# Six of POOL's convolution additions per batch issued as accumulating DMA transfers from a product buffer of their own, in a two-layer attention and convolution kernel

## The chip, the cores and the metric

The kernel runs on one core of a Trainium2 chip. The metric is the device time of one execution, in microseconds (us). The engines are PE (matrix products), DVE (vector), ACT (scalar), POOL (GpSimd) and SP, which issues the loads and stores. They run side by side, each through its own list of instructions in order, and meet at semaphores.

## The reference

The input is x, 4 images of 256 channels by 32 x 32 pixels, all float32. Layer one computes per batch image:

```python
q, k, v = h @ wq.T, h @ wk.T, h @ wv.T                      # 768 channels in all
dw = conv(qkv, dw_kernel, 5x5, 'SAME', one filter per channel)
pw = conv(dw, pw_kernel, 1x1, groups of 8 channels)
qkv_all = concat([qkv, pw])                                 # linear attention of 8-channel heads, with relu
out = (scores @ query)[:-1] / (denominator + EPS)
y = batchnorm(conv1x1(out, proj_kernel)) + x
```

Layer two is a full attention over the 1,024 pixels: y is normalized per channel, energy = F^T G (1024 x 1024), softmax over its rows, the result multiplied by H(y), one more 1x1 convolution, plus y. The part that the change touches is `dw`, the depthwise 5 x 5 convolution: 25 taps for each of 768 channels, each a shifted image times one number per channel, added up.

## The kernel before

The 768 channels are six tiles of 128 partitions. `raw` holds the images with a border, `conv` the sums. For each tile 25 taps are to be added up, and they are shared out by tile. DVE does tiles 2, 3, 0 and most of 1 with one multiply-and-add each. For tiles 4 and 5 and for 17 taps of tile 1, ACT writes a product (image times weight) into one of the buffers `prod`, and POOL adds it to a sum. Ten of these 17 (`LATE`) are added to a tile `late` of their own, which lies in `rows`; the other seven are the taps (1, 10) to (1, 16), here called the shared taps. Tap (1, 10) is written straight to `conv` by ACT and starts the sum, and the six others are additions of POOL. DVE takes that sum as the start of its own part, taps (1, 17) to (1, 24).

`POOL_SEQ` is the list of 57 products of a batch: the taps of tiles 4 and 5 in turn, with the shared taps put in at places 32, 34, ..., 44. ACT makes the products in that order, at most `PROD_BUFS` additions ahead of POOL, and POOL adds them in that order. In the first batch PE does tile 5 and ten taps of tile 0 with diagonal matrices (`diagonal_conv`), so that the list `FIRST_POOL_SEQ` is shorter.

The batches overlap. The body of batch b on each engine ends layer one, does layer two and, between its own steps, the convolution of batch b + 1. How many products ACT makes behind each of its steps is written out by hand in tables such as these two, for the eight row blocks (0 to 7) of layer two's softmax:

```python
PRODUCTS_EXP = (2, 3, 4, 1, 1, 2, 1, 0, 0, 1)
PRODUCTS_ATT = (1, 2, 2, 1, 1, 4, 3, 5, 0, 3)
```

In this loop block i goes through `energy` on PE (L533), a row maximum on DVE (L1116), the exponential on ACT (L900), transposes on PE (L546), their copies `pt` on ACT (L909), `values` on PE (L555), and a final operation on DVE (L1133). Products 30 and 31 come after the first exponential, 32 to 34 after the second, 35 after the first pair of `pt` copies, 36 to 39 after the third exponential, 40 and 41 after the second pair of copies, 42 after the fourth exponential, 43 and 44 after the third pair of copies.

PE begins layer one's end (`body`, L578) of a batch only when POOL has done all of its `conv` additions. POOL's nine late additions follow, and PE waits for them before it multiplies `late` (L595).

The order on each engine is the order of the code. No scheduler is between.

Of the kernel before, what the change touches and what calls it, by code (L numbers as in the profile page):

```python
# [6 lines left out]
ALU = mybir.AluOpType  # L7
# [5 lines left out]
P = 128  # L13
# [3 lines left out]
N = SIDE * SIDE  # L17
# [31 lines left out]
SHARED_TILE = 1  # L49
# [3 lines left out]
LATE = 10  # L53
SHARED_TAPS = 7

PROD_BUFS = 5

KV_TILES = (2, 4, 5, 3)
Q_TILES = (0, 1)
# [9 lines left out]
CARRY = 18  # L69


def pool_order(taps):

    own = [(t, i) for i in range(NTAPS) for t in POOL_TILES]
    for i in range(SHARED_TAPS):
        own.insert(SHARED_AT + 2 * i, (SHARED_TILE, LATE + i))
    return [tap for tap in own if tap in taps]
# [4 lines left out]
POOL_SEQ = pool_order(ALL_TAPS)  # L82
FIRST_POOL_SEQ = pool_order([tap for tap in ALL_TAPS if tap not in PE_TAPS])
DVE_SEQ = [(t, i) for t in DVE_TILES for i in range(NTAPS) if (t, i) not in POOL_SEQ + LATE_SEQ]
DVE_TAPS, PRODUCTS = len(DVE_SEQ), len(POOL_SEQ)
# [2 lines left out]
assert DVE_SEQ.index(PE_SHARED_END) < DVE_TAPS - CARRY  # L88

POOL_STARTS = [(t, 0) for t in POOL_TILES] + [(SHARED_TILE, LATE)]  # L90
ADD_SEQ = [tap for tap in POOL_SEQ if tap not in POOL_STARTS]
FIRST_ADD_SEQ = [tap for tap in FIRST_POOL_SEQ if tap not in POOL_STARTS]
POOL_ADDS = len(ADD_SEQ)


# [50 lines left out]
def conv_seq_kernel(nc, x, wqkv, dw, pw, proj, bn, fgw, hw, ow, l1b, masks, out):  # L146
    with ExitStack() as ctx:
        def sb(name, shape, dt=F32):
            return ctx.enter_context(nc.sbuf_tensor(name, shape, dt))

        def sem(name):
            return ctx.enter_context(nc.semaphore(name))
# [7 lines left out]
        conv = sb("conv", [P, TILES, N])  # L160
        rows = sb("rows", [P, ROW_BUFS, N])
        q_raw = sb("q_raw", [P, 2, CK, N])
        prod = sb("prod", [P, PROD_BUFS, N])
        pt = sb("pt", [P, PT_BUFS, NB, P])
        kt = sb("kt", [P, RB, C])
        vt = sb("vt", [P, RB, CK, SCW + 1])
# [79 lines left out]
        bc_part = sem("bc_part")  # L246
        conv_dve = sem("conv_dve")
        prod_ready = sem("prod_ready")
        conv_pool = sem("conv_pool")
        dve_step = sem("dve_step")  # L250
        res_biased = sem("res_biased")
# [46 lines left out]
        def dve_count(b, n):  # L298
            return DVE_TAPS * b + n


        def product_count(b, n):
            return len(FIRST_POOL_SEQ) + (PRODUCTS + LATE) * b - PRODUCTS + n

        def add_count(b, n):
            return len(FIRST_ADD_SEQ) + (POOL_ADDS + LATE - 1) * b - POOL_ADDS + n

# [3 lines left out]
        def late_add_count(b, n):  # L311
            return add_count(b, POOL_ADDS) + n
# [27 lines left out]
        def image_drained(b, t):  # L340

            return (A_AT["raw_q", b] + 2 * (Q_TILES.index(t) + 1) if t in Q_TILES
                    else A_AT["raw_kv", b] + 2 * (KV_TILES.index(t) + 1))

        def conv_read(b, t):

            return A_AT["pwq", b] + A_PWQ if t in Q_TILES else A_AT["pwkv", b] + A_PWKV
# [6 lines left out]
        def square(image):  # L354
            return image.rearrange("p (y x) -> p y x", x=SIDE)
# [387 lines left out]
        def _(act):  # L743
# [20 lines left out]
            def conv_products(b, first, last):  # L764

                seq, adds = (POOL_SEQ, ADD_SEQ) if b else (FIRST_POOL_SEQ, FIRST_ADD_SEQ)
                for n in range(first, min(last, len(seq))):
                    t, i = seq[n]
                    if (t, i) in POOL_STARTS:
                        act.wait_ge(a_free, image_drained(b, t))  # L770
                        if b:
                            act.wait_ge(a_full, conv_read(b - 1, t))
                        dst, part = conv[:, t, :], False
                    else:
                        m = adds.index((t, i))

                        if b:
                            act.wait_ge(conv_pool, add_count(b, max(m - PROD_BUFS + 1, 0)))
                        elif m >= PROD_BUFS:
                            act.wait_ge(conv_pool, m - PROD_BUFS + 1)  # L780
                        dst, part = prod[:, m % PROD_BUFS, :], True
                    product(dst, t, i, part)
# [7 lines left out]
            def late_products(b, first, last):  # L790

                for n in range(first, min(last, LATE)):
                    if n > 0:

                        act.wait_ge(conv_pool, late_add_count(b, max(n - PROD_BUFS, 0)))
                    product(late if n == 0 else prod[:, (n - 1) % PROD_BUFS, :], *LATE_SEQ[n], n > 0)
# [130 lines left out]
            done = [0]  # L927
# [31 lines left out]
        def _(dve):  # L959
# [17 lines left out]
            def conv_taps(b, first, last):  # L977

                for n in range(first, last):
                    t, i = DVE_SEQ[n]  # L980
                    if b == 0 and (t, i) in PE_TAPS:
                        continue
                    if n == 0 or DVE_SEQ[n - 1][0] != t:
                        dve.wait_ge(a_free, image_drained(b, t))
                    if n > 0 or b:

                        skipped = PE_SHARED_TAPS if b == 0 and (t, i) == PE_SHARED_END else 0
                        dve.wait_ge(conv_dve, dve_count(b, n - skipped))
                    if i == NTAPS - 1 and b:
                        dve.wait_ge(a_full, conv_read(b - 1, t))  # L990
                    final = square(conv[:, t, :])
                    if SHARED_TAPS and t == SHARED_TILE and i == LATE + SHARED_TAPS:

                        adds = ADD_SEQ if b else FIRST_ADD_SEQ
                        done = adds.index((t, i - 1)) + 1
                        if n >= DVE_TAPS - CARRY:
                            done = POOL_ADDS if b else len(FIRST_ADD_SEQ)
                        dve.wait_ge(conv_pool, add_count(b, done) if b else done)
                        tap(acc, t, i, final).then_inc(conv_dve, 1)
                    elif b == 0 and (t, i) == PE_SHARED_END:  # L1000

                        dve.wait_ge(a_free, A_AT["conv_shared", 0] + A_CONV)
                        tap(acc, t, i, final).then_inc(conv_dve, 1 + PE_SHARED_TAPS)
                    else:
                        starts = n == 0 or DVE_SEQ[n - 1][0] != t
                        tap(final if i == NTAPS - 1 else acc, t, i, None if starts else acc).then_inc(conv_dve, 1)
# [168 lines left out]
        @block.gpsimd  # L1175
        def _(pool):
            def rstd(b, c):
                pool.wait_ge(var_ready, CK * b + c + 1)
                pool.tensor_tensor(stat_rstd[:, c:c + 1], stat_ve[:, c:c + 1], minus_half[:, c:c + 1],  # L1179
                                   ALU.pow).then_inc(rstd_ready, 1)  # L1180

            def add(total, m, i):

                total, product = inner(square(total), i), inner(square(prod[:, m % PROD_BUFS, :]), i)
                pool.tensor_tensor(total, total, product, ALU.add).then_inc(conv_pool, 1)  # L1185

            def conv_adds(b, first, last):

                seq, adds = (POOL_SEQ, ADD_SEQ) if b else (FIRST_POOL_SEQ, FIRST_ADD_SEQ)
                for m in range(first, min(last, len(adds))):  # L1190
                    t, i = adds[m]
                    n = seq.index((t, i)) + 1
                    pool.wait_ge(prod_ready, product_count(b, n) if b else n)

                    if (t, i - 1) in adds:
                        before = adds.index((t, i - 1)) + 1
                        pool.wait_ge(conv_pool, add_count(b, before) if b else before)
                    add(conv[:, t, :], m, i)

            def late_adds(b):  # L1200

                for m in range(LATE - 1):
                    pool.wait_ge(prod_ready, late_product_count(b, m + 2))
                    if m > 0:
                        pool.wait_ge(conv_pool, late_add_count(b, m))
                    add(late, m, LATE_SEQ[m + 1][1])

            pool.memset(raw[:], 0.0).then_inc(images_cleared, 1)

            pool.wait_ge(constants_set, 1)  # L1210
            pool.wait_ge(bn_ve_ready, 1)
            pool.tensor_tensor(bn_tmp, bn_ve, minus_half, ALU.pow).then_inc(bn_rstd_ready, 1)
            conv_adds(0, 0, 4)
            split_lo(pool, 1)
            conv_adds(0, 4, POOL_ADDS)
            for b in range(B):
                late_adds(b)
                if b + 1 < B:
                    conv_adds(b + 1, 0, RSTD_AT[0])
                rstd(b, 0)  # L1220
                if b + 1 < B:
                    conv_adds(b + 1, RSTD_AT[0], RSTD_AT[1])
                rstd(b, 1)
                if b + 1 < B:
                    conv_adds(b + 1, RSTD_AT[1], POOL_ADDS)
                if b + 2 < B:
                    split_lo(pool, b + 2)
# [51 lines left out]
```

## Time and profile before

| what | value |
| --- | --- |
| median of 3 runs | 764.02 us (763.96 to 765.4) |
| the profiled execution | 763.93 us |
| its span in the profile | 762.1 us |
| PE, DVE, ACT, POOL busy | 676.1, 571.2, 457.2, 531.4 us |
| POOL's `conv` additions | 192, 422.2 us |
| ACT's products | 228 into `prod`, 245.8 us |

The span is the time from the first to the last recorded instruction; 1.8 us of the profiled execution lie outside it. Busy times overlap, so that they do not add up to the span, and an engine that is idle often waits for another. Bodies 0, 1 and 2 look alike: the same steps come again 164.0 us later.

### The profile page before, as it was taken

What the parts mean: (1) busy time and instruction counts of PE and PEld (TensorE: products, weight loads), DVE (VectorE), ACT (ScalarE), POOL (GpSimd) and SP (SyncE); (2) the same over time, 40 slices, a digit from 0 to 9 for tenths busy, and PEclk for the clock granted to TensorE, in tenths of its full rate; (3) what the DMA queues carried; (4) which work ended last, traced back from release to release, by engine and by line L of the source; (5) the groups of instructions that cost most, each with busy time, mean ns of one, the idle gap of its engine ahead of it and who ended that gap; (6) DMA issues with size and microseconds to landing.
All of it is one profiled execution on the core that took longest, in us unless ns stands there. A gap on an engine that the chain in (4) does not pass through costs nothing.

```text
span 762.1 us, 8782 instructions
## 1 busy us (share of the span) xinstructions
PE 676.1 (89%) x3276; PEld 501.4 (66%) x3276; DVE 571.2 (75%) x694; ACT 457.2 (60%) x695; POOL 531.4 (70%) x248
## 2 busy tenths in 40 slices
PE   4999979988989999988988999898898975988998
PEld 3944448764857788655767887557577862376787
DVE  6999458996889979978699879978799884342221
ACT  4763447795468569784767777974676772122331
POOL 3469696796898999797789998796989974000000
PEclk9999977999999999999899999999899998797999
DMA  7000000001100000001100000000100000000000
GB/s 273 1 0 1 0 22 34 1 1 44 68 1 11 17 15 15 1 0 56 56 0 15 15 29 0 1 1 1 55 1 15 28 15 0 1 1 0 1 28 28
DMA packets 4938, 16.25 MB, mean 21 GB/s; under 512 B 800, under 2 KB 928, under 8 KB 3872
## 3 DMA queue, kind: packets, MB, share of 16 engines
q1 hardware_dynamic: 4896, 15.69, 5.5%
q8 instruction: 26, 0.43, 0.2%
q14 instruction: 16, 0.13, 0.1%
HBM read 11.50 MB, written 4.19 MB: 21 GB/s over the span
## 4 chain that ended last, share of the span: by engine, by line
PE 53%; DVE 20%; ACT 12%; POOL 9%; issue 3%; DMA 1%; POOLq 0%; SPq 0%; DVEq 0%; ACTq 0%
DVE ps L975 10%; PE ps L555 10%; POOL rows L1185 9%; PE ps L533 8%; PE ps L467 7%; PE ps L615 5%; ACT prod L788 4%; PE ps L566 3%; DVE small L1116 3%; PE ps L654 2%; PE ps L546 2%; PE ps L476 2%; PE ps L423 2%; PE ps L517 2%; PE ps L424 2%
## 5 line engine op out<-in xcount | busy, mean ns | idle before, releaser
L1185 POOL TENSOR_TENSOR conv<-conv,prod 128x930 f32<-128x930 f32 (+4 forms) x192 | 422.2, 2233 | 56.1 <-ACT prod L788 52.2
L975 DVE SCALAR_TENSOR_TENSOR ps<-raw,dw_sb,ps 128x960 f32<-128x960 f32 (+4 forms) x290 | 348.3, 1201 | 7.7
L788 ACT ACTIVATE prod<-raw,dw_sb 128x930 f32<-128x930 f32 (+4 forms) x228 | 245.8, 1139 | 10.5 <-POOL conv L1185 10.5
L555 PE MATMUL ps<-ht,pt 128*128 128x256 f32 x512 | 115.7, 380 | 1.6 <-ACT pt L909 1.6
L555 PEld LDWEIGHTS ps<-ht,pt 128*128 128x128 f32 x512 | 94.9, 190 | 14.0 <-ACT pt L909 2.4
L1185 POOL TENSOR_TENSOR rows<-rows,prod 128x930 f32<-128x930 f32 (+4 forms) x36 | 83.7, 2325 | 15.0 <-ACT prod L788 10.4
L900 ACT ACTIVATE rows<-ps,small 128x1024 f32<-128x1024 f32 x32 | 35.6, 1114 | 90.0 <-DVE small L1120 89.8
L533 PE MATMUL ps<-hi,t_hi 128*128 128x512 f32 x128 | 44.8, 431 | 17.8 <-ACT rows L900 17.8
L1116 DVE TENSOR_REDUCE small<-ps 128x1 f32<-128x1024 f32 x32 | 39.0, 1220 | 27.3 <-PE ps L533 27.3
L423 PE MATMUL ps<-hi,wqkv_hi 128*128 128x512 f32 x96 | 39.1, 407 | 10.4 <-DVE lo L325 10.2
L803 ACT ACTIVATE kt<-ps 128x256 f32<-128x256 f32 x68 | 31.9, 470 | 26.8 <-PE ps L578 23.4
L1133 DVE SCALAR_TENSOR_TENSOR x_t<-ps,small,x_t 128x256 f32<-128x256 f32 x32 | 15.3, 477 | 43.1 <-PE ps L555 43.1
L533 PEld LDWEIGHTS ps<-hi,t_hi 128*128 128x128 f32 x128 | 23.1, 190 | 27.7 <-ACT rows L900 18.6
L533 PE MATMUL ps<-lo,t_hi 128*128 128x512 f32 x128 | 41.1, 403 | 0.0
L1179 POOL TENSOR_TENSOR small<-small 128x1 f32<-128x1 f32 x8 | 4.4, 548 | 51.0 <-DVE small L1068 51.0
L476 PE MATMUL ps<-vt,kt 128*128 128x129 f32 x272 | 33.6, 285 | 7.1 <-DVE rows L1030 4.5
L476 PEld LDWEIGHTS ps<-vt,kt 128*128 128x128 f32 x272 | 32.9, 200 | 9.1 <-issue 6.0
L424 PE MATMUL ps<-hi,wqkv_lo 128*128 128x512 f32 x96 | 38.0, 396 | 0.0
L566 PE MATMUL ps<-oh_w,x 128*128 128x256 f32 x128 | 30.0, 384 | 7.8 <-DVE lo L1070 7.6
L546 PE MATMUL ps<-mask_sb,rows 128*128 128x128 f32 x256 | 34.0, 276 | 3.1 <-ACT pt L909 3.1
L546 PEld LDWEIGHTS ps<-mask_sb,rows 128*128 128x128 f32 x256 | 29.4, 142 | 10.3 <-issue 5.4
L533 PE MATMUL ps<-hi,t_lo 128*128 128x512 f32 x128 | 35.5, 400 | 0.0
(135 smaller groups left out, 1113.7 us busy)
## 6 DMA issues: line engine op xcount, KB each, us to landing
q_raw<-x_dram SPq DMA_DIRECT2D x4, 1024.0 KB, 5.7
x<-x_dram SPq DMA_DIRECT2D x4, 1024.0 KB, 4.8
out_dram<-x_t SPq DMA_DIRECT2D x16, 256.0 KB, 2.3
conv<-wqkv_dram SPq DMA_DIRECT2D x1, 768.0 KB, 4.5
conv<-fg_dram SPq DMA_DIRECT2D x1, 512.0 KB, 5.7
proj_sb<-proj_dram SPq DMA_DIRECT2D x1, 512.0 KB, 7.4
pw_sb<-pw_dram SPq DMA_DIRECT2D x1, 384.0 KB, 6.7
mask_sb<-masks_dram SPq DMA_DIRECT2D x1, 264.0 KB, 6.2
```

The costliest lines, as they stand in the source:

```text
L423: pe.matmul(dst, lh, rh, start=(k == 0), stop=False)
L424: pe.matmul(dst, ll, rh, start=False, stop=False)
L467: mm = pe.matmul(dst, diagonal(t, i), view, start=(i == 0), stop=(i == taps - 1))
L476: mm = pe.matmul(dst[:, h * C:h * C + SCW], kt[:, j, h * P:(h + 1) * P], vt[:, j, h, 0:SCW], start=(j == 0), stop=(j == blocks - 1))
L533: mm = pe.matmul(ps[:, E_PAIR + h, :], lhs, m[:, h * HALF:(h + 1) * HALF], start=(s == 0), stop=(s == len(steps) - 1))
L546: mm = pe.transpose(ps[:, T_PAIR + u, j * P:(j + 1) * P], rows[:, i % ROW_BUFS, key:key + P], ident)
L555: mm = pe.matmul(dst[:, 0:C], pt[:, i % PT_BUFS, j, :], ht[:, j, :], start=(j == 0), stop=(j == NB - 1))
L566: mm = pe.matmul(dst[:, i * C:(i + 1) * C], x1[:, k, n], oh_w[:, k, :], start=(k == 0), stop=(k == CK - 1))
L788: act.activation(dst, view, ACT.Copy, scale=weight(t, i)).then_inc(prod_ready, 1)
L975: return dve.scalar_tensor_tensor(dst, view, w, before, ALU.mult, ALU.add)
L1116: dve.tensor_reduce(neg_max[:, i:i + 1], ps[:, E_PAIR:E_PAIR + 2, :].rearrange("p a n -> p (a n)"), AX.X, ALU.max, negate=True).then_inc(r ...
L1185: pool.tensor_tensor(total, total, product, ALU.add).then_inc(conv_pool, 1)
```

## The change

The six additions of taps (1, 11) to (1, 16) are taken from POOL's list of additions. ACT writes the product of such a tap, now the whole 1,024 columns, into one buffer `prod_dma`, and POOL issues a DMA transfer of 512 KB that adds this buffer to tile 1 of `conv`. There is one such buffer. So ACT waits, before it writes each of these products, until the transfer before it has landed (`dma_added`), and POOL waits for the same before it issues the next. The buffers for the other products go from five to four. DVE's tap (1, 17) waits for all six transfers in place of POOL's additions.

```diff
-PROD_BUFS = 5
+PROD_BUFS = 4
...
-ADD_SEQ = [tap for tap in POOL_SEQ if tap not in POOL_STARTS]
-FIRST_ADD_SEQ = [tap for tap in FIRST_POOL_SEQ if tap not in POOL_STARTS]
+DMA_SEQ = [(SHARED_TILE, LATE + i) for i in range(1, SHARED_TAPS)]
+ADD_SEQ = [tap for tap in POOL_SEQ if tap not in POOL_STARTS + DMA_SEQ]
+FIRST_ADD_SEQ = [tap for tap in FIRST_POOL_SEQ if tap not in POOL_STARTS + DMA_SEQ]
...
+        prod_dma = sb("prod_dma", [P, N])
...
+                    elif (t, i) in DMA_SEQ:
+                        before = len(DMA_SEQ) * b + DMA_SEQ.index((t, i))
+                        if before > 0:
+                            act.wait_ge(dma_added, 16 * before)
+                        dst, part = prod_dma[:], False
...
-                        adds = ADD_SEQ if b else FIRST_ADD_SEQ
-                        done = adds.index((t, i - 1)) + 1
-                        if n >= DVE_TAPS - CARRY:
-                            done = POOL_ADDS if b else len(FIRST_ADD_SEQ)
-                        dve.wait_ge(conv_pool, add_count(b, done) if b else done)
+                        dve.wait_ge(dma_added, 16 * len(DMA_SEQ) * (b + 1))
...
+            def dma_add(b, tap, seq):
+
+                n = seq.index(tap) + 1
+                pool.wait_ge(prod_ready, product_count(b, n) if b else n)
+                before = len(DMA_SEQ) * b + DMA_SEQ.index(tap)
+                if before > 0:
+                    pool.wait_ge(dma_added, 16 * before)
+                pool.dma_start(conv[:, tap[0], :], prod_dma[:], accum_op=ALU.add).then_inc(dma_added, 16)
+
             def conv_adds(b, first, last):
...
+                    since = seq.index(adds[m - 1]) + 1 if m else 0
+                    for tap in seq[since:n]:
+                        if tap in DMA_SEQ:
+                            dma_add(b, tap, seq)
                     pool.wait_ge(prod_ready, product_count(b, n) if b else n)
```

On POOL, in a batch after the first, from the last addition before the shared taps on: `conv<-conv,prod` is an addition. Before:

```order
L1185 TENSOR_TENSOR conv<-conv,prod 128x992 [waits conv_pool,prod_ready]
L1185 TENSOR_TENSOR conv<-conv,prod 128x32x30 [waits prod_ready]
L1185 TENSOR_TENSOR conv<-conv,prod 128x992 [waits conv_pool,prod_ready]
L1185 TENSOR_TENSOR conv<-conv,prod 128x32x31 [waits conv_pool,prod_ready]
L1185 TENSOR_TENSOR conv<-conv,prod 128x31x31 [waits conv_pool,prod_ready]
L1185 TENSOR_TENSOR conv<-conv,prod 128x32x30 [waits conv_pool,prod_ready]
L1185 TENSOR_TENSOR conv<-conv,prod 128x31x31 [waits conv_pool,prod_ready]
```

And now:

```order
L1189 TENSOR_TENSOR conv<-conv,prod 128x992 [waits conv_pool,prod_ready]
L1198 DMA conv<-prod_dma 128x1024 [waits dma_added,prod_ready]
L1189 TENSOR_TENSOR conv<-conv,prod 128x992 [waits conv_pool,prod_ready]
L1198 DMA conv<-prod_dma 128x1024 [waits dma_added,prod_ready]
L1189 TENSOR_TENSOR conv<-conv,prod 128x31x31 [waits conv_pool,prod_ready]
L1198 DMA conv<-prod_dma 128x1024 [waits dma_added,prod_ready]
L1189 TENSOR_TENSOR conv<-conv,prod 128x31x31 [waits conv_pool,prod_ready]
```

Every second instruction has become a DMA issue, which waits for the one before it to have landed; one addition stands between two of them.

On ACT, in the softmax loop of the first body, from the second exponential (`rows,small<-ps,small`) on; the first `conv<-raw` is product 32, and `pt<-ps` are the copies for PE. The same stretch of the later bodies is alike:

```order
L796 ACTIVATE conv<-raw,dw_sb 128x1024 [waits a_full,a_free]
L796 ACTIVATE prod<-raw,dw_sb 128x992 [waits conv_pool]
L796 ACTIVATE prod_dma<-raw,dw_sb 128x1024 [waits dma_added]
L917 COPY pt<-ps 128x512 [waits t_full] x2
L796 ACTIVATE prod<-raw,dw_sb 128x992 [waits conv_pool]
L908 ACTIVATE rows,small<-ps,small 128x1024 [waits max_ready]
L796 ACTIVATE prod_dma<-raw,dw_sb 128x1024 [waits dma_added]
L796 ACTIVATE prod<-raw,dw_sb 128x31x31 [waits conv_pool]
L796 ACTIVATE prod_dma<-raw,dw_sb 128x1024 [waits dma_added]
L796 ACTIVATE prod<-raw,dw_sb 128x31x31 [waits conv_pool]
L917 COPY pt<-ps 128x512 [waits t_full] x2
```

The order of ACT's work is the same as before. Six of its products go to `prod_dma` and have a new wait, and the exponentials and the copies stand behind them.

On ACT, in the first batch, from the copies of PE's first diagonal convolution on. Before:

```order
L820 COPY conv<-ps 128x512 [waits a_full] x2
L788 ACTIVATE prod<-raw,dw_sb 128x32x30 [waits conv_pool]
L788 ACTIVATE prod<-raw,dw_sb 128x32x31 [waits conv_pool]
L788 ACTIVATE prod<-raw,dw_sb 128x31x31 [waits conv_pool]
L788 ACTIVATE prod<-raw,dw_sb 128x32x30 [waits conv_pool]
L788 ACTIVATE prod<-raw,dw_sb 128x31x30 [waits conv_pool] x2
L788 ACTIVATE prod<-raw,dw_sb 128x31x31 [waits conv_pool]
L820 COPY conv<-ps 128x512 [waits a_full] x2
L788 ACTIVATE prod<-raw,dw_sb 128x992 [waits conv_pool]
```

And now:

```order
L828 COPY conv<-ps 128x512 [waits a_full] x2
L796 ACTIVATE prod_dma<-raw,dw_sb 128x1024
L796 ACTIVATE prod_dma<-raw,dw_sb 128x1024 [waits dma_added]
L796 ACTIVATE prod<-raw,dw_sb 128x31x31 [waits conv_pool]
L796 ACTIVATE prod_dma<-raw,dw_sb 128x1024 [waits dma_added] x2
L796 ACTIVATE prod<-raw,dw_sb 128x31x30 [waits conv_pool]
L796 ACTIVATE prod_dma<-raw,dw_sb 128x1024 [waits dma_added]
L828 COPY conv<-ps 128x512 [waits a_full] x2
L796 ACTIVATE prod_dma<-raw,dw_sb 128x1024 [waits dma_added]
```

Five of the six transfers' products now stand ahead of the copies of the second diagonal convolution, and the sixth right behind them.

## Rows read from the trace of the kernel before

**Rows 1.** The page: busy time by engine, and the chain that ended last.

```profile
PE 676.1 (89%) x3276; PEld 501.4 (66%) x3276; DVE 571.2 (75%) x694; ACT 457.2 (60%) x695; POOL 531.4 (70%) x248
...
PE 53%; DVE 20%; ACT 12%; POOL 9%; issue 3%; DMA 1%; POOLq 0%; SPq 0%; DVEq 0%; ACTq 0%
```

**Rows 2.** The chain in order of time: start us, us, what.

```profile
284.71 0.91 PE ps L578 x8
...
287.33 0.95 ACT prod L788
...
288.36 2.15 POOL rows L1185
...
308.31 2.26 POOL rows L1185
```

**Rows 3.** Who waited for whom: us in total, times, longest us.

```profile
POOL conv L1185 <- ACT prod L788: 52.2, 25, 8.5
...
ACT prod L788 <- POOL conv L1185: 10.5, 7, 3.9
```

**Rows 4.** POOL's timeline: start us, us, what, idle before it.

```profile
230.59 52.76 POOL L1185 TENSOR_TENSOR conv<-conv,prod 128x992 f32<-128x992 f32 x24 [3.06 <-ACT prod L788]
283.30 4.68 POOL L325 TENSOR_TENSOR lo<-q_raw,hi 128x1024 fp32r<-128x1024 f32 x2
```

**Rows 5.** ACT's timeline in the softmax loop of the first body.

```profile
229.40 2.12 ACT L788 ACTIVATE prod<-raw,dw_sb 128x992 f32<-128x992 f32 x2
...
234.66 4.12 ACT L788 ACTIVATE prod<-raw,dw_sb 128x992 f32<-128x992 f32 x4
238.69 1.06 ACT L909 COPY pt<-ps 128x512 f32<-128x512 f32 x2
...
252.51 1.11 ACT L900 ACTIVATE rows<-ps,small 128x1024 f32<-128x1024 f32 x1 [3.79 <-DVE small L1120]
```

**Rows 6.** The page's DMA issues: count, KB each, us to landing.

```profile
x<-x_dram SPq DMA_DIRECT2D x4, 1024.0 KB, 4.8
out_dram<-x_t SPq DMA_DIRECT2D x16, 256.0 KB, 2.3
```

**Rows 7.** The loads of `q_raw`: duration ns min/median/max of the issue, and landing.

```profile
L372 SPq DMA_DIRECT2D q_raw<-x_dram x4: 327/382/463, 1.2 to 351.3; - x4
...
DMA to landing us min/median/max: 4.8/5.7/9.4
```

**Rows 8.** The first batch, timelines of ACT, POOL and PE.

```profile
82.94 7.07 ACT L788 ACTIVATE prod<-raw,dw_sb 128x960 f32<-128x960 f32 x7
...
98.45 0.58 ACT L820 COPY conv<-ps 128x512 f32<-128x512 f32 x1 [7.77 <-PE ps L467]
...
107.19 0.37 ACT L809 COPY s_t<-ps 128x256 f32<-128x256 f32 x1 [2.32 <-PE ps L485]
...
84.12 15.74 POOL L1185 TENSOR_TENSOR conv<-conv,prod 128x960 f32<-128x960 f32 x7 [6.06 <-ACT prod L788]
...
110.34 6.85 POOL L1185 TENSOR_TENSOR conv<-conv,prod 128x930 f32<-128x930 f32 x3 [0.48 <-POOL conv L1185]
...
117.79 9.67 PE L578 MATMUL ps<-pw_sb,conv 128*128 128x128 f32 x64
```

**Rows 9.** The chain again: two blocks of `energy` on PE.

```profile
215.21 2.98 PE ps L533 x12
...
221.03 4.62 PE ps L533 x12
```

**Rows 10.** Busy time in stretches: PE, PEld, DVE, ACT, POOL; then granted clock, DMA.

```profile
220.00:226.00 6.00, 4.96 (x16) 3.64 (x16) 3.65 (x5) 2.99 (x4) 6.00 (x4) 0.72 0.00 0
226.00:232.00 6.00, 5.01 (x28) 3.33 (x24) 5.89 (x8) 4.75 (x7) 2.94 (x2) 1.00 0.00 0
```

**Rows 11.** DVE's timeline: nine taps beside POOL's additions, nine taps without.

```profile
285.15 11.09 DVE L975 SCALAR_TENSOR_TENSOR ps<-raw,dw_sb,ps 128x961 f32<-128x961 f32 x9
...
309.37 11.10 DVE L975 SCALAR_TENSOR_TENSOR ps<-raw,dw_sb,ps 128x900 f32<-128x900 f32 x9
```

More of the change, by code:

```diff
@@ L248, in conv_seq_kernel @@
         prod_ready = sem("prod_ready")
+        dma_added = sem("dma_added")
         conv_pool = sem("conv_pool")
```

## Prediction

> **What bounds the kernel now.** I read the page first. No engine is busy all the time: PE is at 89%, POOL at 70%. The chain that ended last lies on PE for 53% of the span, on DVE for 20%, on ACT for 12% and on POOL for 9% [rows 1]. So a microsecond taken from POOL counts only where POOL is on the chain.
>
> The chain in order of time shows where that is: in the nine late additions, from 288.36 to 310.57 [rows 2]. Those are not changed. They begin 0.07 us after the first late product has ended on ACT (287.33 + 0.95 = 288.28), and that product waits for PE's new batch, whose first products of L578 start at 284.71 [rows 2]. POOL's `conv` additions, from which six are taken, end at 283.3 (230.59 + 52.76, 24 of them, 2.20 us each), and what POOL does next ends at 288.0 [rows 4]. They are early. The waits agree: POOL waited 52.2 us for products, ACT only 10.5 us for free buffers [rows 3].
>
> ACT is different. In the softmax loop each exponential and each pair of `pt` copies is a link between DVE and PE, and the products stand between them [rows 5]. Whatever holds ACT there for longer than its idle time (3.79 us before the exponential at 252.51 [rows 5]) holds PE and DVE behind it.
>
> **What is removed.** Six additions of 2.20 us in each of four batches: 24 x 2.20 = 52.8 us of POOL [rows 4]. None of it is on the chain, so I book 0.
>
> **What is added: a loop through the DMA.** Call L the time from POOL's issue of a transfer to its landing. With one buffer, the next product for it can only start on ACT when the transfer has landed, and the next transfer starts when that product is there. The products take 1.03 us (4.12 / 4 [rows 5]); with some 0.1 us for the two semaphore steps I take 1.15 us. Six transfers need five such rounds of L + 1.15 us between the first issue and the end of the sixth product. ACT works in order, so exponentials and copies wait too.
>
> *Bodies 0 to 2,* which make the products of batches 1 to 3. The first such product (34) ends at 231.5 (229.40 + 2.12), but POOL is at the addition of product 33, which starts at 230.59 and takes 2.20 [rows 4, 5]. Thus the first issue is at 232.85. The sixth product (44) ends at 232.85 + 5 (L + 1.15), and the exponential of block 4 (blocks counted from 0) follows right after it, where it was at 252.51 [rows 5]. The delay is 5L - 13.9 us. In the rounds the other work of ACT (at most two copies, 1.06 us, a product and an exponential, 1.11 us) fits into L, the row maximum of block 4 is ready long before, and POOL has one addition (2.20 us) to do per round, which fits too. From that exponential on the loop goes as before: PE is full there, and nothing gives the time back. POOL has twelve `conv` additions left behind the sixth transfer, 12 x 2.2 = 26.4 us, and waits some 3 to 4 us for products among them; it ends about 15 us later than the 283.3 of before, and the L578 of PE (284.71 before) comes 16 us later for L = 6. POOL is again just ahead, by about 1 us.
>
> *The first batch.* The first of these products ends at 84.1, when POOL is waiting for it (its row starts at 84.12) [rows 8]. The fifth ends at 84.1 + 4 (L + 1.15), and the copy of the second diagonal convolution, which ended at 99.0, stands behind it. The sixth ends at 84.1 + 5 (L + 1.15). Behind it POOL has the issue and six additions, 2.3 us each as in its last row there (6.85 / 3) [rows 8], and PE may start L578 when they are done: 84.1 + 5L + 5.75 + 1.1 + 13.8 = 104.8 + 5L against 117.8 before [rows 8]. The delay is 5L - 13.0. The way over the copy and `s_t` (107.19) is a little shorter.
>
> Three bodies make products for a next batch, so the sum is (5L - 13.0) + 3 (5L - 13.9) = 20L - 54.7 us.
>
> **L.** The trace has no accumulating transfer and none issued by POOL, so I bound it. From 256 KB in 2.3 us and 1,024 KB in 4.8 [rows 6], a plain copy of 512 KB would take 2.3 + 256 x 2.5 / 768 = 3.1 us: the lower end. An accumulating one must read product and sum, 1 MB, and write 512 KB. Its nearest row is the 1 MB load: 4.8 us. To this comes the issue. SP's takes 0.33 to 0.46 us [rows 7]; POOL's I put midway between this and the 2.2 us at which issuing would cost as much as adding, 1.2 us. That gives L = 6.0. The upper end is the slowest load, 9.4 us [rows 7]. With L = 6.0 the delays are 17.0 + 3 x 16.1 = 65.3 us; with 3.1, 7.3 us; with 9.4, 133.3 us.
>
> The Trainium skill (DMA: Bandwidth & Descriptors, Anatomy of one DMA) fits transfers from POOL by 2.0 us plus bytes over 436 GB/s. For 512 KB that would be an estimated 3.2 us, and by the sum above 9.3 us in all. It does not say what accumulation adds; no row here shows it.
>
> **The clock.** After PE had waited 1.5 us for an exponential, one block of `energy` took 4.62 us where another took 2.98 [rows 9], and the granted clock of that stretch was 0.72, which mixes the levels of 1.2 and 2.4 GHz; then 1.00 [rows 10]. PE will now idle several us in each of the three loops, and I book one such block each: 3 x 1.6 = 4.9 us.
>
> **Other parts.** Four buffers for five: ACT waited for POOL 10.5 us in all, seven times [rows 3], in the first batch while PE's diagonal products (until 98.45 [rows 8]) set the pace. Later POOL's queue holds fewer additions than before. I book 0; should it reach the chain once in each batch, it costs one addition, 2.2 us, four times. Products of 1,024 columns in place of 930 or 992: below 0.1 us each, inside the 1.15. DVE's tap (1, 17) needs the sixth transfer, which lands over 20 us before it is reached: 0; were that cover gone, DVE would wait for what is missing of L.
>
> **Sum.** 763.9 + 65.3 + 4.9 = 834 us. The profiled execution (763.93) is 0.1 us from the median, so this stands for the median too.
>
> **The rivals.**
> *Light transfers.* L between 2.8 and 4.5. For it: 3.1 us by the rows of plain copies, and most of the reading might be hidden. Against: twice the bytes to read and an issue in software. At 3.5 the sum is 15.3 + 2 to 5 for the clock, about 783 us.
> *Heavy transfers.* L above 7.5, if adding in the transfer runs slower than copying. For it: a landing of 9.4 exists in the rows. Against: it was in a crowd of loads at the start, here the DMA engines are nearly idle. At 8.5: 115.3 + 5, about 884 us.
> *Hidden.* If L is at most 2.7, the rounds take less than the time ACT and the others need anyway, and 5L - 13.9 is below zero: no change, 764. It needs a landing near that of a 256 KB store.
> *Faster.* With L under 2.7 and POOL's additions gone, DVE's taps beside them could get quicker, if the two engines hold each other up. DVE has some twenty taps on the chain in each of three loops; 0.05 us for each would give 3 us, 761. Against: nine taps take 11.09 us beside POOL's additions and 11.10 without [rows 11]. And L decides it: above 2.9 the loops cost more than these 3 us.
>
> **How the numbers follow.** Chances: L from 4.5 to 7.5 (799 to 864 us) 0.55; light 0.22, heavy 0.18, hidden 0.02, faster 0.03. The likeliest gives 834. The range must leave out no more than 2 in 10: from 788 (L = 3.7, the middle of the light case) to 890 (L = 8.8). A measurement of this kernel tells about 0.2%, 1.5 us, from no change. Slower 0.95, same 0.02, faster 0.03.
>
> **What would show it.** Right: ACT's products into `prod_dma` wait for DMA, 20 times for about 4 to 6 us; the exponential of block 4 comes 16 us later against the loop's start; a body takes about 182 us in place of 164.0; POOL is busy some 50 us less and idle for more; DMA issues of POOL land after about 6 us. Wrong, if the landing is not 6 us (each us off moves the sum by 20); if ACT's waits are short but the time grows, then another engine took the wait, POOL first; if PE's `energy` blocks take 5 us throughout the loop, the clock costs more than one block.

## The result and the profile after

The changed kernel takes 820.11 us (median of 4 runs, 819.08 to 823.44), the kernel before, run beside it, 764.71 us (4 runs, 763.96 to 767.28). The ratio is 1.0726, with a 95% interval of 1.0684 to 1.0768. So it is slower by 7.3%, 55 us. The prediction was 834 us, 788 to 890.

The page of the changed kernel, parts 1, 4, 5 and 6, as in [rows 1, 6]; the profiled execution took 823.44 us with a span of 821.6:

```profile
PE 698.3 (85%) x3276; PEld 517.6 (63%) x3276; DVE 577.1 (70%) x694; ACT 459.4 (56%) x695; POOL 499.4 (61%) x248
...
PE 40%; issue 18%; DVE 14%; DMA 12%; ACT 10%; POOL 6%; POOLq 0%; SPq 0%; DVEq 0%; ACTq 0%
...
L796 ACT ACTIVATE prod_dma<-raw,dw_sb 128x1024 f32<-128x1024 f32 x24 | 27.6, 1148 | 69.6 <-DMA conv<-prod_dma 69.6
L1198 POOL DMA_DIRECT2D conv<-prod_dma x24 | 21.4, 892 | 70.7 <-ACT prod_dma L796 70.7
...
conv<-prod_dma POOLq DMA_DIRECT2D x24, 512.0 KB, 4.6
```

POOL did lose work: 531.4 us became 499.4. It did 24 additions less (422.2 us of `conv` additions became 371.6), and 24 issues of 21.4 us in all, which partly overlap the additions behind them, took back 18.6 us of that. DMA, 1% of the chain before, is now 12% of it, and "issue", the time in which an engine waited for nothing that the profile shows, went from 3% to 18%. Part of it is the other half of the loop through the DMA, 20 times some 1.5 us (elsewhere the chain books POOL's own additions as issue, so the 18% is no measure of the waits). The chain in order of time shows it. Its rows in the softmax loop of the first body (start us, us, what):

```profile
245.74 4.53 DMA conv<-prod_dma
250.27 0.03 issue
250.29 0.02 POOLq L1197
250.31 1.56 issue
251.87 0.02 POOLq L1214
251.89 4.56 DMA conv<-prod_dma
...
257.92 4.58 DMA conv<-prod_dma
...
264.06 5.10 DMA conv<-prod_dma
...
270.63 4.54 DMA conv<-prod_dma
...
276.25 1.19 ACT rows L908 x2
277.44 0.04 issue
277.49 4.27 PE ps L536 x12
```

One pattern repeats here: five transfers, and between each and the next 1.5 to 1.6 us of product and semaphores. Only behind the last does the chain come back to the exponential of L908 (L900 before) and to PE. ACT's timeline of the same loop, the counterpart of [rows 5], gives the same from the waiting side (idle before an instruction in brackets):

```profile
240.15 1.12 ACT L908 ACTIVATE rows<-ps,small 128x1024 f32<-128x1024 f32 x1 [4.26 <-DVE small L1124]
...
250.29 1.16 ACT L796 ACTIVATE prod_dma<-raw,dw_sb 128x1024 f32<-128x1024 f32 x1 [2.63 <-DMA conv<-prod_dma]
...
256.47 1.15 ACT L796 ACTIVATE prod_dma<-raw,dw_sb 128x1024 f32<-128x1024 f32 x1 [4.03 <-DMA conv<-prod_dma]
...
275.19 1.15 ACT L796 ACTIVATE prod_dma<-raw,dw_sb 128x1024 f32<-128x1024 f32 x1 [2.91 <-DMA conv<-prod_dma]
276.25 1.09 ACT L908 ACTIVATE rows<-ps,small 128x1024 f32<-128x1024 f32 x1
```

The exponential of block 4, at 276.25, no longer waits for DVE: it has no idle time of its own, since ACT has only just come free. From block 1 (240.15) to it there are 36.1 us. Before there were 25.26.

Who waited for whom (us in total, times, longest), the counterpart of [rows 3]:

```profile
POOL conv L1198 <- ACT prod_dma L796: 70.7, 21, 6.3
ACT prod_dma L796 <- DMA conv<-prod_dma: 69.6, 20, 5.0
DVE x_t L1137 <- PE ps L558: 68.8, 26, 8.0
```

The 20 new waits of ACT hold 69.6 us. POOL waits as long for ACT (70.7). The delay is handed on: PE's waits for ACT's `pt` copies grew from 3.1 us to 28.8, and DVE's for PE from 43.1 to 68.8.

I measure where the time went by the start of POOL's nine late additions in each batch. Before, they start at 122.68, 288.36, 452.38 and 615.55, and the span ends at 762.1. After, at 135.66, 313.70, 491.74 and 668.60, and the end is 821.6. So the first batch is 13.0 us longer, the three bodies that make products for a next batch 12.4, 14.0 and 13.7, and the last body, which makes none, 6.4. The sum is 59.5 us, the difference of the spans. (The medians differ by 55; the profiled execution of the changed kernel is 3.3 us above its median, that of the kernel before 0.8 below.)

### The profile page after: what moved, and what is told of

It reads as the page before. It is cut to its first block, busy times and chain, and to the rows that moved or that the text cites. A ratio compares the mean times of both kernels' runs of the same rounds, so it can differ in the third digit from the quotient of the medians.

```text
span 821.6 us, 8785 instructions
## 1 busy us (share of the span) xinstructions
PE 698.3 (85%) x3276; PEld 517.6 (63%) x3276; DVE 577.1 (70%) x694; ACT 459.4 (56%) x695; POOL 499.4 (61%) x248
## 4 chain that ended last, share of the span: by engine, by line
PE 40%; issue 18%; DVE 14%; DMA 12%; ACT 10%; POOL 6%; POOLq 0%; SPq 0%; DVEq 0%; ACTq 0%
DMA conv<-prod_dma 11%; PE ps L558 8%; DVE ps L983 8%; PE ps L536 6%; PE ps L470 5%; POOL conv L1189 4%; ACT prod L796 3%; PE ps L618 3%; PE ps L479 3%; POOL rows L1189 3%; PE ps L594 2%; PE ps L520 2%; PE ps L426 2%; PE ps L549 2%; PE ps L427 1%
## 5 line engine op out<-in xcount | busy, mean ns | idle before, releaser
L1189 POOL TENSOR_TENSOR conv<-conv,prod 128x930 f32<-128x930 f32 (+4 forms) x168 | 371.6, 2235 | 67.3 <-ACT prod L796 63.8
L796 ACT ACTIVATE prod<-raw,dw_sb 128x930 f32<-128x930 f32 (+4 forms) x204 | 221.8, 1137 | 14.4 <-POOL conv L1189 13.4
L558 PE MATMUL ps<-ht,pt 128*128 128x256 f32 x512 | 121.3, 393 | 1.6 <-ACT pt L917 1.6
L558 PEld LDWEIGHTS ps<-ht,pt 128*128 128x128 f32 x512 | 99.4, 199 | 15.5 <-ACT pt L917 2.4
L908 ACT ACTIVATE rows<-ps,small 128x1024 f32<-128x1024 f32 x32 | 35.5, 1110 | 79.7 <-DVE small L1124 79.6
L796 ACT ACTIVATE prod_dma<-raw,dw_sb 128x1024 f32<-128x1024 f32 x24 | 27.6, 1148 | 69.6 <-DMA conv<-prod_dma 69.6
L1198 POOL DMA_DIRECT2D conv<-prod_dma x24 | 21.4, 892 | 70.7 <-ACT prod_dma L796 70.7
L1137 DVE SCALAR_TENSOR_TENSOR x_t<-ps,small,x_t 128x256 f32<-128x256 f32 x32 | 15.4, 480 | 68.8 <-PE ps L558 68.8
L549 PE MATMUL ps<-mask_sb,rows 128*128 128x128 f32 x256 | 36.9, 292 | 28.8 <-ACT pt L917 28.8
L426 PE MATMUL ps<-hi,wqkv_hi 128*128 128x512 f32 x96 | 39.6, 412 | 10.5 <-DVE lo L328 10.3
L479 PE MATMUL ps<-vt,kt 128*128 128x129 f32 x272 | 39.5, 315 | 7.1 <-DVE rows L1034 4.5
L479 PEld LDWEIGHTS ps<-vt,kt 128*128 128x128 f32 x272 | 38.8, 230 | 9.1 <-issue 6.0
L536 PE MATMUL ps<-lo,t_hi 128*128 128x512 f32 x128 | 43.7, 425 | 0.0
```

What stands on the lines that cost most here:

```text
L426: pe.matmul(dst, lh, rh, start=(k == 0), stop=False)
L479: mm = pe.matmul(dst[:, h * C:h * C + SCW], kt[:, j, h * P:(h + 1) * P], vt[:, j, h, 0:SCW], start=(j == 0), stop=(j == blocks - 1))
L536: mm = pe.matmul(ps[:, E_PAIR + h, :], lhs, m[:, h * HALF:(h + 1) * HALF], start=(s == 0), stop=(s == len(steps) - 1))
L549: mm = pe.transpose(ps[:, T_PAIR + u, j * P:(j + 1) * P], rows[:, i % ROW_BUFS, key:key + P], ident)
L558: mm = pe.matmul(dst[:, 0:C], pt[:, i % PT_BUFS, j, :], ht[:, j, :], start=(j == 0), stop=(j == NB - 1))
L796: act.activation(dst, view, ACT.Copy, scale=weight(t, i)).then_inc(prod_ready, 1)
```

## The experiments

The kernel before took 767.38 us (median of 13 runs, 760.6 to 771.26) beside the first four kernels, and 768.7 us (19 runs, 760.98 to 771.08) beside the last four; each ratio is to the runs beside it.

**Two buffers for the transfers' products.** The edit, against the changed kernel:

```diff
-PROD_BUFS = 4
+PROD_BUFS = 3
...
-        prod_dma = sb("prod_dma", [P, N])
+        prod_dma = sb("prod_dma", [P, 2, N])
...
-                        if before > 0:
-                            act.wait_ge(dma_added, 16 * before)
-                        dst, part = prod_dma[:], False
+                        if before > 1:
+                            act.wait_ge(dma_added, 16 * (before - 1))
+                        dst, part = prod_dma[:, before % 2, :], False
...
-                pool.dma_start(conv[:, tap[0], :], prod_dma[:], accum_op=ALU.add).then_inc(dma_added, 16)
+                pool.dma_start(conv[:, tap[0], :], prod_dma[:, before % 2, :], accum_op=ALU.add).then_inc(dma_added, 16)
```

> The changed kernel with two buffers for the transfers' products and three for the others, so that it uses the same memory and issues the same 24 transfers in the same places. A product then waits for the transfer before the last. Theory (rounds through one buffer hold ACT): transfers follow each other about 4.7 us apart in place of 6.1, the sixth product comes some 12 us earlier in each batch, block 4 of the softmax loop is less than 2 us late, and the time is 765 to 775 us. Rival (the transfers themselves disturb, by 0.9 us of issue on POOL, by traffic or by delayed additions): the same 24 of them are there, so the time stays above 800. Rival (too few product buffers): it gets worse than 820, since three are fewer than four.

It took 783.3 us, ratio 1.0205 (1.0145 to 1.0264): 8 us above the range of the expectation. POOL's timeline shows what is left:

```profile
244.39 0.91 POOL L1198 DMA_DIRECT2D conv<-prod_dma  x1 [1.98 <-DMA conv<-prod_dma]
245.02 2.56 POOL L1189 TENSOR_TENSOR conv<-conv,prod 128x961 f32<-128x961 f32 x1
249.49 0.90 POOL L1198 DMA_DIRECT2D conv<-prod_dma  x1 [1.92 <-DMA conv<-prod_dma]
250.11 2.56 POOL L1189 TENSOR_TENSOR conv<-conv,prod 128x961 f32<-128x961 f32 x1
254.72 0.89 POOL L1198 DMA_DIRECT2D conv<-prod_dma  x1 [2.05 <-DMA conv<-prod_dma]
```

The product is out of the loop, but POOL still waits for each transfer before it issues the next one to the same sum. No run leaves that wait out. On average they are 5.1 us apart in the first batch and 5.2 to 5.3 in the bodies, in place of 6.1 to 6.2. Now it is POOL that waits for landings (42.1 us), and ACT 34.7 us in place of 69.6. The late additions come 8.2 us late in the first batch, the bodies are 0.5, 2.6 and 3.9 us longer, and the last one 3.5. Waiting through one buffer was thus over two thirds of the loss (2.0% is left of 7.3%); the serial transfers are a loop of their own. Not all that is left is theirs: with three product buffers ACT waits for POOL's `conv` additions 30.6 us (13.4 in the changed kernel). The two weren't tested apart.

**A plain copy in place of the accumulating transfer.** This one leaves six taps of tile 1 out of the sum.

```diff
-                pool.dma_start(conv[:, tap[0], :], prod_dma[:], accum_op=ALU.add).then_inc(dma_added, 16)
+                pool.dma_start(conv[:, tap[0], :], prod_dma[:]).then_inc(dma_added, 16)
```

> The changed kernel with plain copies of the same 512 KB in place of accumulating transfers; so six taps' sum on tile 1 is left out (each copy overwrites). Theory: only the landing changes. By plain copies of the kernel before it would be 3.1 to 3.7 us in place of 4.6, and 20 rounds give 20 x 0.9 to 1.5 = 18 to 30 us less than 820: 790 to 802. Rival (issue and number of transfers count, not their length): no change from 820.

**A quarter of the width.** It accumulates 256 of the 1,024 columns and leaves the rest of these six products out.

```diff
-                pool.dma_start(conv[:, tap[0], :], prod_dma[:], accum_op=ALU.add).then_inc(dma_added, 16)
+                pool.dma_start(conv[:, tap[0], 0:256], prod_dma[:, 0:256], accum_op=ALU.add).then_inc(dma_added, 16)
```

> The changed kernel with accumulating transfers of only the first 256 columns of the product, 128 KB in place of 512; three quarters of the six taps' sums are left out. Theory: landing falls to about 2.5 to 3 us, 20 rounds give 32 to 42 us less than 820: 778 to 788. Rival (fixed cost per transfer rules): landing above 4 us and time above 805.

The copy took 787.68 us, ratio 1.025 (1.0198 to 1.0303), the quarter 781.19, ratio 1.0162 (1.0115 to 1.0209). Here are the issue (ns, min/median/max) and the landing of the changed kernel:

```profile
L1198 POOL DMA_DIRECT2D conv<-prod_dma x24: 859/884/1039, 85.4 to 632.6; - x24
DMA to landing us min/median/max: 4.5/4.6/5.2
```

of the plain copy:

```profile
L1198 POOL DMA_DIRECT2D conv<-prod_dma x24: 530/580/722, 84.9 to 599.7; - x24
DMA to landing us min/median/max: 2.9/2.9/5.5
```

and of the quarter:

```profile
L1198 POOL DMA_DIRECT2D conv<-prod_dma x24: 862/887/1042, 85.0 to 591.9; - x24
DMA to landing us min/median/max: 2.6/2.7/4.5
```

Accumulation adds 1.7 us to the landing of 512 KB, of which 0.3 us is the issue; the accumulating issue of a quarter of the width is as long as that of the whole. The copy's rounds are mostly 4.3 to 4.7 us long, but one transfer in each body landed late, after 5.32, 5.48 and 4.48 us. The first two were under way when SP issued a store of 256 KB to `out_dram` (at 253.28 and 423.56), the third was not, so the cause stays open. From first issue to last, the 20 rounds take 95.3 us in place of the changed kernel's 123.0: 28 us less. By the two ratios the copy gained 4.8% of 765, 36 us, a little more than the 18 to 30 expected. The prediction's sum, which has 20 times L, would give 34 for these 1.7 us; so the total fits it better than the rounds do. And at L = 2.9 the sum gives 3.3 us of loss, while the copy lost 20. With the rounds as measured it gives 17.6. The quarter lies where it was expected.

**The transfers spread over the loop**, six places apart from place 14 of the list on, in place of two apart from place 32 on:

```diff
-SHARED_AT = 32
+SHARED_AT = 14
...
-        own.insert(SHARED_AT + 2 * i, (SHARED_TILE, LATE + i))
+        own.insert(SHARED_AT + 6 * i, (SHARED_TILE, LATE + i))
```

> The changed kernel with the seven shared taps put in at places 14, 20, ..., 50 of the list of products in place of 32, 34, ..., 44. One buffer, 24 accumulating transfers of 512 KB as before. Theory: between two of these products there are now five others, some 11 us of POOL, more than a round of 6.1 us, so that nearly no product waits for a landing: 762 to 768 us, and POOL's relief brings nothing, since it is not on the path. Rival (transfers themselves cost): above 800. Rival (POOL's relief is worth something once the waits are gone): below 760.

It took 768.6 us (10 runs), ratio 1.0013 (0.9985 to 1.004): no difference from before, as expected. Its waits and POOL's busy time:

```profile
ACT prod_dma L796 <- DMA conv<-prod_dma: 14.1, 3, 8.3
```
```profile
PE 681.7 (88%) x3276; PEld 504.5 (65%) x3276; DVE 576.8 (75%) x694; ACT 458.2 (59%) x695; POOL 499.1 (65%) x248
```

The transfers, their landing (4.6 us) and the one buffer are as in the changed kernel. Only the places of the transfers differ, and the whole loss is gone. The three waits that are left all lie in the first batch, where some transfers are still 6.0 to 6.2 us apart; in the bodies they are 11.4 to 16.1 us apart. The same kernel shows that 32 us less on POOL bring nothing that could be seen: the interval goes from 1 us faster to 3 us slower.

**The parts that were booked at nothing.** Four product buffers in the kernel before, and then the shared taps spread in the kernel before, with POOL adding them:

```diff
-PROD_BUFS = 5
+PROD_BUFS = 4
```

> The kernel before with four product buffers in place of five, and nothing else. Theory (rounds through one transfer buffer explain the slowdown): the fifth buffer is off the path, within 2 us of before. Rival (part of the slowdown is the lost buffer): slower by 5 us or more.

The second edit is that of the spread transfers, made to the kernel before.

> The kernel before, with POOL adding all taps, and the shared taps at places 14, 20, ..., 50 as in the spread version. It shows what the places alone do. Theory: within 3 us of before and of the spread version with transfers (ratio to before 1.001), since neither places nor transfers are on the path then. Rival (places cost and transfers give it back, or the other way round): this one differs from the spread version with transfers by more than 4 us.

They took 768.4 us, ratio 0.9997 (0.9968 to 1.0026), and 767.0 us, ratio 0.9998 (0.9959 to 1.0038). With four buffers ACT waits for POOL 22.1 us in place of 10.5 [rows 3], and nothing comes of it. Both are as expected. The order alone changes nothing either, so the spread transfers owe nothing to their places in the list as such.

**Spending the relief.** If POOL's list is short, two of its nine late additions, which are on the chain [rows 2], can be moved into the shared taps. I did this with the spread transfers, which makes them eight per batch, and with POOL adding. The edit, against the changed kernel and the kernel before:

```diff
-LATE = 10
-SHARED_TAPS = 7
+LATE = 8
+SHARED_TAPS = 9
...
-SHARED_AT = 32
+SHARED_AT = 14
...
-        own.insert(SHARED_AT + 2 * i, (SHARED_TILE, LATE + i))
+        own.insert(SHARED_AT + 5 * i, (SHARED_TILE, LATE + i))
```

> The spread version with transfers, and two taps moved from the late sum to the shared one: LATE 8 for 10, SHARED_TAPS 9 for 7, places 14, 19, ..., 54. POOL has seven late additions on the path in place of nine, and DMA has eight additions per batch. Theory: the late additions ended 3 us after DVE's own last tap (310.6 against 307.6), so that each of bodies 0 to 2 gains about 3 us and no more: 9 us in all, ratio to before 0.985 to 0.992. Rival (no gain, since what POOL gives up comes back elsewhere, for instance waits for landings, 5 places apart): 1.00 or above.

> The same move of two taps, LATE 8 and SHARED_TAPS 9 at places 14, 19, ..., 54, with POOL doing all additions itself as before. Theory: POOL's conv additions then end 4.4 us later (287.7) and what follows ends at 292.4, 4 us after the late additions could start, so that the 4.8 us saved in them are nearly given back: within 3 us of before. Then the gain of the version with transfers is due to the relief of POOL. Rival: as fast as the version with transfers; then the relief is worth nothing and the move of taps is all.

With transfers it took 776.51 us (773.2 to 777.95), ratio 1.0118 (1.0064 to 1.0173). With POOL adding it took 779.83 (776.14 to 782.85), ratio 1.0153 (1.0098 to 1.0208). The gain of some 9 us did not come, and the second, expected within 3 us of before, is 11 us slower. POOL's timeline shows that the late additions did get shorter, 17.34 us in place of 22:

```profile
290.21 17.34 POOL L1189 TENSOR_TENSOR rows<-rows,prod 128x900 f32<-128x900 f32 x7
316.89 4.27 POOL L1189 TENSOR_TENSOR conv<-conv,prod 128x900 f32<-128x900 f32 x2 [9.34 <-ACT prod L796]
```

POOL is done at 307.6 and then idles for 9.34 us. The chain has gone to DVE, whose taps run without a gap from 285.59 on:

```profile
285.59 1.14 DVE ps L983
...
298.00 2.77 DVE ps L983
...
308.13 1.29 DVE conv L983
309.43 0.14 issue
309.56 2.81 PE ps L594 x6
```

The expectation left out what PE does in between. In the kernel before, DVE's last tap ends at 307.6, as it says, and POOL's late additions at 310.57 [rows 2]. But PE has six products of `conv` to do (L591, L594 above) before it needs `late`. PE's timeline of the kernel before:

```profile
307.74 2.81 PE L591 MATMUL ps<-conv,pw_sb 128*128 128x512 f32 x6 [0.37 <-DVE conv L975]
310.61 1.12 PE L595 MATMUL ps<-rows,pw_sb 128*128 128x512 f32 x2
```

These six are done at 310.55. The way over DVE and the way over POOL thus reached L595 within 0.1 us of each other, and the room was not 3 us but nearly nothing. That is where the gain went. Besides, DVE's way got longer: tap (1, 17), 1.29 us in this batch before, took 2.77 on this chain, and 2.71 to 2.77 in each of the four batches (the last section comes back to it). PE is at L598 (L595 before) at 312.37, 1.8 us later than before; 0.4 of it is DVE's later start, 1.5 the tap. The bodies take 166.5 to 167.5 us with transfers and 169.6 to 170.3 with POOL adding, against 163.2 to 165.7 before. With POOL adding, its longer list is on the chain: its `conv` additions end at 291.3, and PE's L578 starts at 291.57, which was 284.71 [rows 2]. With transfers, POOL's `conv` additions and issues wait 108.6 us for ACT's products, 90.8 in the spread kernel. What the rest of the loss of 8 to 11 us is I did not separate. Between the two kernels the transfers are ahead by 3.3 us, but their runs overlap, so this is not settled.

## Why the prediction was right, step by step

**The bound and the relief.** Right. POOL's additions of `conv` were off the path: without them the time is the same (the spread transfers).

**The loop through the DMA.** Right in kind and place: 20 waits, five in each of four batches, of 3.5 us on average where I had 4 to 6; block 4's exponential held, by 10.8 us in place of 16; a body of 178.0 us in place of 182. From that exponential on the chain runs over PE and ACT; POOL's `conv` additions end at 308.36, 1.7 us ahead of the L581 of PE (L578 before), so that POOL was just ahead, as I had it. POOL is busy 32 us less, not some 50, because its issues count. The spread transfers and the two buffers confirm it from two sides. The rivals *hidden* and *faster* fall with the result. The rival *light* (L between 2.8 and 4.5) misses L by 0.1 us only, but its 783 us are far from the time. *Heavy* is out by the landing.

**L, the term that was mis-sized.** I took 6.0 us. The transfer took 4.6 from its issue to its landing, of which POOL's issue is 0.89 (I had put 1.2 for it on top of a landing of 4.8). The bounds 3.1 and 9.4 held. (In the chances, the 799 us that go with L = 4.5 lack the clock's 4.9.) The plain copy confirms the lower row: 2.9 us against my 3.1. The Trainium skill (DMA: Bandwidth & Descriptors, Anatomy of one DMA) gives an estimate of 3.2 us for 512 KB; the trace comes near it for a copy, 2.9 us, and not for an accumulation, 4.6 us, of which the section says nothing.

**The round.** I added 1.15 us to L for product and semaphores. The chain shows 1.47 to 1.62. Five rounds of 6.1 to 6.2 us on average in place of my 7.15 make the prediction's delays 11.6 us in the first batch and about 11 in the others, where I had 17.0 and 16.1. The two errors in L and in the rest of the round are of opposite sign, -1.4 and +0.4; over 20 rounds, -28 and +8 us.

**The clock.** Booked 1.6 us for each of three loops. After the exponential of block 4, one block of `energy` took 4.27 us, as the chain above shows, against 3.02 for the same block before. Stretches of busy time inside the rounds and, last, across that block (PE, PEld, DVE, ACT, POOL; then granted clock):

```profile
250.00:256.00 6.00, 2.33 (x11) 1.57 (x9) 5.89 (x6) 2.15 (x2) 3.17 (x2) 0.92 0.46 87
256.00:262.00 6.00, 2.77 (x11) 2.62 (x12) 2.74 (x5) 3.10 (x4) 3.17 (x2) 0.50 0.46 87
262.00:268.00 6.00, 6.00 (x22) 4.87 (x21) 1.23 (x2) 3.21 (x4) 3.10 (x2) 0.72 0.46 87
...
280.00:286.00 6.00, 6.00 (x28) 5.16 (x27) 3.88 (x5) 2.94 (x5) 3.09 (x3) 0.80 0.12 22
```

PE is busy for 2.33 us and for 2.77 us of two stretches of 6, and in the second the granted clock is 0.50, that is 1.2 GHz. Across the block it is 0.80. From block 4 to the late additions the loop takes 37.45 us, before 35.85: 1.6 us, as booked, and the chain has all of it in that block and the transposes behind it (1.24 in place of 0.87). With 11 for the rounds this gives 12.6 for the first of the bodies, and 12.4 was measured.

**What was not foreseen.** The sum with these measured terms is 11.6 + 3 x 12.7 = 49.7 us, and the spans differ by 59.5. What is missing is 1.4 us in the first batch (1.3 of it lies before the rounds: the first transfer is issued at 85.39, where I had 84.1; ACT's copy ahead of its product, which waits for PE's diagonal products, starts at 83.44, before at 82.45), 1.3 and 1.0 in the second and third body, and 6.4 in the last body, which has no transfer in it. The last body takes 153.0 us, before 146.5. But four-buffer and spread kernels, which are as fast as the kernel before, show 150.0 us (four buffers), 146.3 (spread, POOL adding) and 152.7 (spread, transfers, profiled in the slowest of its ten runs) for the same body. So this is hardly a cost of the waits.

Two things are seen in it. One is DVE's tap (1, 17), booked at 0, in the last body of the changed kernel:

```profile
677.89 3.21 DVE L983 SCALAR_TENSOR_TENSOR ps<-raw,dw_sb,conv 128x1024 f32<-128x1024 f32 x1
```

The transfers had landed long before, as I had argued, but the tap took 3.21 us in place of 1.29. It took 3.21 us in the spread transfers too, 2.02 in the spread kernel with POOL adding, and 1.29 with four buffers, whose last body was long all the same. The tap alone therefore doesn't explain the 6.4 us. It is on the chain, though, and so are PE's six products behind DVE's taps. The chain of the changed kernel:

```profile
677.89 3.22 DVE ps L983
...
689.90 5.46 PE ps L594 x6
```

and of the kernel before:

```profile
624.71 1.30 DVE ps L975
...
634.80 4.38 PE ps L591 x6
```

These two rows are 1.9 and 1.1 us longer. The six products point to the other thing, the clock: in the first 40 us stretch after the late additions start, the granted clock is 0.74 in the changed kernel (669 to 709) and 0.82 in the kernel before (616 to 656). Over the whole last body it is 0.91 in the two profiles where this body takes some 146 us (before; spread, POOL adding), and 0.86 to 0.88 in the six where it takes 149 to 153 (four buffers, two buffers, copy, quarter, spread transfers, changed). The runs of the kernel before spread over 1.4%, 760.6 to 771.3, which has room for most of what is missing. Whether the change makes such a last body more likely stays open: each kernel has one profile, and I made no run for it.

In the plain copy and the quarter the measured rounds give 17.6 and 9.4 us by the prediction's sum, and the last bodies are 4.2 and 2.8 us longer; their spans are 24.6 and 16.1 us above the 762.1 of before. Body by body the sum does not fit: the copy's bodies should be 5.0, 5.1 and 4.3 us longer and are 3.1, 6.3 and 7.0. In the quarter's first body the chain leaves the transfers after the second and runs over PE and DVE, so the rounds no longer set the pace there. This remainder I can't assign to a step.

**Luck.** The prediction was 14 us over the median. L, 1.4 us too long, put it 28 us too high; the rest of the round took back 8, and the 9.8 us that the sum doesn't contain, the last body's 6.4 above all, took back more. The median is 3.3 us below the profiled execution. That these offset half of the error in L is luck.

## What to carry to other kernels

Work that is moved to a DMA queue can cost the round trip, not only the transfer. Ask which in-order engine waits for it (here ACT, which also carries the exponentials), how many round trips follow one another, and what that engine would have done between two of them: six transfers 11 to 16 us apart in each body cost nothing that the runs could show, the same six two places apart cost 12 to 14 us a batch. A second buffer takes only the producer out of the loop; transfers into one sum that wait for each other still stand in line. And before relief is spent on a stretch where one engine sets the end, follow the next engine's way to the same point with all that stands on it: here the six products of PE behind DVE's last tap left less than 0.1 us.

## What the runs showed of the hardware

An accumulating transfer of 512 KB within SBUF took 4.6 us (median; up to 5.2, and to 6.0 in the spread kernel), a plain one 2.9 us (up to 5.5), and one of 128 KB that accumulates 2.7 us. POOL was held 0.89 us by the issue of an accumulating transfer of either size, and 0.58 us by that of a copy, against 2.2 us for the addition itself. In the two kernels with spread transfers some issues took up to 1.45 and 1.48 us.

DVE's tap (1, 17), whose two large inputs `raw` and `conv` both lie in SBUF, took 1.29 us, or up to 3.40 us (with fewer late additions, POOL adding) beside POOL's late additions. Where it is short, one of POOL's additions can be long. In the second batch's late additions of the kernel before, DVE's timeline and the chain have:

```profile
297.65 1.29 DVE L975 SCALAR_TENSOR_TENSOR ps<-raw,dw_sb,conv 128x1024 f32<-128x1024 f32 x1
```
```profile
297.75 3.23 POOL rows L1185
```

DVE starts 0.1 us ahead and takes 1.29; POOL's addition takes 3.23 in place of 2.2 to 2.3.

The other taps, which have one large input in PSUM, take 1.2 us and show nothing of the kind. The Trainium skill (SBUF — State Buffer, Who interferes with whom) says that DVE's second pair of ports is shared with GpSimd (POOL) and held by one of them at a time. The trace agrees, with 1 us more for POOL or 2 us more for DVE.
